# A recurrent block with routed experts on one core: the receptance product on VectorE in every step, row scatters in one run per step, expert slots starting two places earlier

## The reference

```python
xn = _layernorm(x, axis=-1)
s = _L0_attn_ref(xn, ...)            # recurrent block
g = _silu(_L0_ffn_ref(xn, ...))      # shared expert + one routed expert per token
x = x + s * g
...
# in _L0_attn_ref
k = einsum(xk, att_kw); v = einsum(xv, att_vw); sr = sigmoid(einsum(xr, att_rw))
rwkv = sr * _wkv(time_decay, time_first, k, v)     # the receptance product
x = x + einsum(rwkv, att_ow)
h = _ln(x, ln2_w, ln2_b)                            # second norm
kk = square(relu(einsum(xk, f_kw))); x = x + sigmoid(einsum(xr, f_rw)) * einsum(kk, f_vw)
# in _L0_ffn_ref: the shared swiglu of all tokens, and for each token
# the swiglu of the expert with the largest logit, on x * sigmoid(logit)
```

## Time and profile before

| | us |
|---|---|
| median of 3 runs | 498.06 |
| the profiled execution, its own time | 497.8 |
| its span, first to last instruction | 495.9 |
| TensorE (PE) busy | 444.2 |
| VectorE (DVE) busy | 406.5 |
| ScalarE (ACT) busy | 355.9 |
| GpSimd (POOL) busy | 282.2 |

### The profile page before, as it was taken

How to read it: one execution, slowest core, us unless ns; L and a number is a source line. 1 busy time by engine, 2 the same in 40 slices (tenths; PEclk the granted TensorE clock), 3 DMA queues, 4 the chain that set the end, 5 groups by cost and what they waited for, 6 DMA issues and landing times. The chain is left out here.

```text
span 495.9 us, 9005 instructions
## 1 busy us (share of the span) xinstructions
PE 444.2 (90%) x2663; PEld 332.7 (67%) x2663; DVE 406.5 (82%) x806; ACT 355.9 (72%) x716; POOL 282.2 (57%) x318
## 2 busy tenths in 40 slices
PE   1898998869989997799999999999999999988895
PEld 1667665547566663669686969687878787855562
DVE  4573969969799797979796979797988989789996
ACT  4868778564565657578787878787879697867891
POOL 7834685288787888427374655555555646470050
PEclk9999899898999999999999999999999999999999
DMA  8992000011511111225757565746573837209397
GB/s 255 273 275 51 2 0 1 5 45 57 190 35 48 46 33 51 55 81 151 212 156 214 172 208 171 232 138 206 147 237 108 226 101 224 79 19 291 106 123 217
DMA packets 66384, 64.97 MB, mean 131 GB/s; under 512 B 5952, under 2 KB 54465, under 8 KB 66256
## 3 DMA queue, kind: packets, MB, share of 16 engines
q1 hardware_dynamic: 58512, 53.52, 38.4%
q0 software_dynamic: 6960, 9.84, 7.3%
q10 hardware_dynamic: 864, 1.04, 0.7%
HBM read 46.86 MB, written 19.28 MB: 133 GB/s over the span
## 5 line engine op out<-in xcount | busy, mean ns | idle before, releaser
L1049 POOL DMA_INDIRECT routed_out<-xh,xs x71 | 93.1, 1312 | 45.2 <-ACT xh L809 30.5
L1041 POOL DMA_INDIRECT tokens_by_expert<-xn,pos x64 | 68.5, 1070 | 27.4 <-issue 27.4
L518 PEld LDWEIGHTS bank_ring<-xh,ew 128*128 128x128 f32 x568 | 70.2, 192 | 10.8 <-issue 9.7
L518 PE MATMUL bank_ring<-xh,ew 128*128 128x128 f32 x568 | 75.6, 276 | 1.0 <-ACT xh L809 0.5
L475 PE MATMUL bank_out<-fvw,kk 128*128 128x128 f32 x512 | 66.1, 277 | 0.0
L475 PEld LDWEIGHTS bank_out<-fvw,kk 128*128 128x128 f32 x512 | 62.0, 193 | 1.9 <-issue 1.9
L1318 DVE TENSOR_TENSOR kk<-rk 128x512 f32<-128x512 f32 x30 | 24.1, 804 | 40.9 <-ACT rk L767 40.7
L801 ACT ACTIVATE px<-bank_ring 128x256 f32<-128x256 f32 x71 | 27.1, 381 | 25.4 <-PE bank_ring L518 25.2
L532 PE MATMUL bank_ring<-ew,hx 128*128 128x128 f32 x284 | 43.5, 276 | 0.4 <-ACT xh L809 0.4
L532 PEld LDWEIGHTS bank_ring<-ew,hx 128*128 128x128 f32 x284 | 37.8, 193 | 0.6 <-ACT xh L809 0.6
L485 PEld LDWEIGHTS bank_ring<-sdn,hs 128*128 128x128 f32 x256 | 31.0, 192 | 10.3 <-issue 6.1
(11 more groups left out here) (198 smaller groups left out, 1096.8 us busy)
## 6 DMA issues: line engine op xcount, KB each, us to landing
ew<-ex_w SPq DMA_DIRECT2D x71, 384.0 KB
tokens_by_expert<-pad_row SPq DMA_DIRECT2D x1, 4686.0 KB, 21.1
xs<-tokens_by_expert SPq DMA_DIRECT2D x71, 66.0 KB, 3.0
xi<-x SPq DMA_DIRECT2D x12, 256.0 KB, 4.6
out<-xn SPq DMA_DIRECT2D x11, 256.0 KB, 4.0
ew<-routed_out SPq DMA_DIRECT2D x9, 256.0 KB, 4.4
out<-x SPq DMA_DIRECT2D x5, 256.0 KB
out<-xn POOLq DMA_DIRECT2D x5, 256.0 KB, 6.0
```

What stands on the lines that cost most here:

```text
L518: last = nc.tensor.matmul(part(GU[n % 2], q, P), part(w, q, P), xt[:, 0:P], start=True, stop=True)
L1041: nc.gpsimd.indirect_dma_start(xs_dram, bass.IndirectOffsetOnAxis(ap=POS[:, t:t + 1], axis=0), XN[:, t * XROW:(t + 1) * XROW], None).then_ ...
L1049: nc.gpsimd.indirect_dma_start(routed_dram, bass.IndirectOffsetOnAxis(ap=XS[(n - 2) % NXS][:, CH:CH + 1].bitcast(i32), axis=0), XH[n % NXH ...
```

## The change

Three edits. `make_rw` goes from GpSimd to VectorE in steps 1 to 14, between `running_max` and the second `ffn_square`. The scatters of a step become one run ahead of place 4: 10 in step 1 and 18 in each of the next three. Slots -2 and -1 move from place (5, 4) to (5, 2), and the others are spread from (5, 3) on instead of (5, 5): 77 places for 73 slots instead of 75.

```diff
     slots = [("E", n) for n in range(-2, XTILES + 2)]
-    steps[E_STEP][4] += slots[:2]
+    steps[E_STEP][2] += slots[:2]
     slots = slots[2:]
-    places = [(E_STEP, k) for k in range(5, 8)] + [(i, k) for i in range(E_STEP + 1, CHUNKS - 1) for k in range(8)]
+    places = [(E_STEP, k) for k in range(3, 8)] + [(i, k) for i in range(E_STEP + 1, CHUNKS - 1) for k in range(8)]
...
-            def make_rw(c):
-                pool.wait_ge(s_tn, c + 1)
-                pool.wait_ge(s_iq, c + 1)
-                if c > 0:
-                    pool.wait_ge(s_att, c)
-                nc.gpsimd.tensor_tensor(RW[:, :], NUM, LQ[:, :], ALU.mult).then_inc(s_rw, 1)
...
-                    scatter(9)
+                    scatter(10)
                 elif 0 < i <= E_STEP:
-                    scatter(12)
+                    scatter(18)
                 for k in range(4, 8):
                     fill(i, k)
-                if T:
-                    make_rw(i)
-                if 0 < i < E_STEP:
-                    scatter(5)
...
                 running_max(2)
+                make_rw(1)
                 ffn_square(0, 3)
...
                 if P1:
                     running_max(i + 1)
+                if T:
+                    make_rw(i)
                 if C:
                     ffn_square(i - 1, 3)
```

## The result

The kernel before took 497.47 us (495.76 to 499.38, 4 runs), the changed one 502.19 us (500.63 to 503.44, 4 runs). The ratio is 1.0094 [1.0053, 1.0136]. The forecast of 492.8 was wrong in its sign, and the time lies outside its range. The profiled execution of the changed kernel took 500.63 us (span 498.7), 2.8 more than the one of before.

What follows compares the result with a forecast made beforehand. TensorE, busy 90%, was to gain from its waits: a lead of 7.7 us by step 5, less 4.7 there, left 3.0; later slots 2.0, sum 5.0 of 497.8, forecast 492.8, range 490.0 to 497.5.

Steps and rivals of the forecast that it cites:

- Step 1, 3.5 and 0.4: End of step 1: product on VectorE removes TensorE's wait, gain 3.5 us; clock staying at 1.00 adds 0.4.
- Steps 2 and 3, 1.4 and nothing: Step 2: product falls into VectorE's idle time and the square's collision goes, gain 1.4 us; step 3 gives nothing.
- Step 4, 1.0 for z and 1.4 for the square: Step 4: TensorE's wait for z and some tenths behind it, 1.0 us; the square's collision with GpSimd's product, 1.4 us.
- the lead is not carried: Rival, chance 0.27: TensorE is full in steps 2 to 4, so only step 1's 3.5 is won; 495.3 us.
- GpSimd keeps pace, at most 1 to 2 us behind the statistics.: Steps sending rows: 18 scatters take about 24 us, x_sm and d 3 more, against steps of 25 to 27.8.
- the long runs of 12 keep 1.26: Argument against the rival that GpSimd falls behind: scatters in the kernel's long runs of 12 stay at 1.26 us.
- the lead of 7.7: Gain in us summed over steps 1 to 4, expected at transpose L400 of step 5, before step 5's give-back.
- The price: GpSimd's scatters: four products and gaps fewer, so the last scatter starts some 6 us earlier, near 191 instead of 197.52.
- the third rival: GpSimd falls behind, chance 0.06: scatters 0.2 us longer each, 3.8 slower, 501.6 us; decides from 0.13 more per scatter.
- The rule on the shared ports: VectorE and GpSimd lock shared ports: three products would each hold a scatter up to 0.69 us; forecast counted no cost.
- The slots, 4.7 in step 5: Step 5: slots moved earlier make TensorE stand; give-back 4.0 us plus a third of 2 us for half clock, 4.7.
- Later, two stretches with a slot fewer, 2.0: After step 5: two stretches between L429s lose a slot, 1.0 us each, gain 2.0, ends 0 and 2.9.

Runs made afterwards that it cites:

- d moved: Changed kernel with old slots, scatters 12, 17, 17, 18, and the time-mixing difference d of chunks 3 to 5 made by VectorE instead of GpSimd: 490.70 us, ratio 0.9872.
- the last two runs there: Chip S: product on VectorE, old slots, scatters 14, 17, 17, 16 (496.47 us); changed kernel with 14 then 17 scatters, step 10's empty place at 2 (498.43).
- the product alone: Kernel before with the product on VectorE, scatters in single runs of 14, 17, 17, 16, slots old: 515.10 us on chip P, 496.47 on chip S.

## Why the prediction was wrong

*Step 1, 3.5 and 0.4.* Right: 3.8 measured, no wait, no square of GpSimd's, clock 1.00.

*Steps 2 and 3, 1.4 and nothing.* Right in sum: 1.0 and 0.6. The products are hidden as said, and the squares are 0.69.

*Step 4, 1.0 for z and 1.4 for the square.* Right as a possibility: with GpSimd relieved (8 or 12 scatters a step, or d moved) steps 1 to 4 took 105.3 to 106.3 us, a lead of 6.7 to 7.8 where the forecast said 7.7. The rival "the lead is not carried", by which steps 2 to 4 would be full on TensorE, is thereby excluded.

*"GpSimd keeps pace, at most 1 to 2 us behind the statistics."* **This is the step that failed.** I counted 24 us for a run of 18, at 1.26 a scatter and with a slow first one, and 3 for x_sm and d, 27 in all; and compared them with steps of 25 to 27.8, where my own sum had just made steps 2 and 4 shorter, by 1.4 and 2.4. Measured, the three runs of 18 took 24.0, 26.0 and 23.4 us, and x_sm and d 4.5, 3.2 and 4.7: 28.6 a step on the mean. Nothing waits in between, so x_sm follows x_sm by 28.5, 29.2 and 28.1, 85.8 together, however fast the others are; steps 2 to 4 took 85.4. The rows of before had it. My argument that "the long runs of 12 keep 1.26" was a wrong reading: from start to start they have 1.38, 1.39 and 1.36 in steps 2 to 4. From the first scatter at 96.01 to the end of the last at 198.48 are 102.5 us, and 64 scatters with their gaps (85.8), three x_sm and d (10.9) and four products (5.8) fill them. GpSimd, 57% busy over the span, was full for those 102 us. Cutting 10, 18, 18, 18 out of 64 put the surplus into step 4; 14, 17, 17, 16 put it into step 2 (32.7); 12, 17, 17, 18 spread it, and 5.5 of the lead of 7.7 are there at step 5, with d moved 7.0.

*The price.* The last scatter started at 194.91, not at 191. I had the four products and their gaps at 6 us; they brought 4.6, since a gap of 0.30 takes the place of each. The first pass ended 0.7 earlier, and longer scatters (1.2) and longer x_sm and d (1.6) took 2.8 back. Step 4's stand of 3.14 and the half clock behind it took 6.2 (31.6 against 25.4), and of the lead of 7.7 at step 5 2.0 were left, 0.7 of them from the first pass. This is the mechanism of the third rival, to which I gave 0.06; it said it decides from 0.13 us more a scatter than 1.26. That is 1.39, which is what they took from start to start over the whole (1088 ns and the gap of 0.30), and in before 1.37. The condition of the rival was as good as met in the trace that I had. That its time of 501.6 comes out as well is luck: it counted 0.2 us more a scatter beside the product, and has nothing of the 2.9 us lost behind step 5.

*The rule on the shared ports.* I set it aside for two scatters of 0.95 and 0.96, and looked only at the new product. The traces bear the rule out, for all of VectorE's instructions with two SBUF inputs. All twenty traces together have 1280 scatters. Of the 554 that begin while VectorE is idle, or in one of its instructions that has a single input or an input in PSUM (a `bank`), none takes over 1.09 us. All 271 that take over 1.12 begin inside one with both inputs in SBUF (`den_num`, the scans of `bb_aa`, `xk`, `kk`, `rw`), and 249 of them are longer than 0.96 by what was left of it, less 0 to 0.25. Of the 299 that begin with 0.35 us or more of such an instruction left, only 53 are not longer, and those began within 0.05 us of its start. The Trainium skill, "SBUF — State Buffer", section "SBUF: two separate sides", has a lock between a VectorE operation with two SBUF inputs and a GpSimd one that reads SBUF; that these scatters are held by it agrees with the numbers above. The new product itself did little: one scatter in steps 2 to 4 begins inside it, that of step 3 at 155.88, 0.35 ahead of its end, and takes 1.18; the one at 129.96 in step 2 begins ahead of it and takes 0.96. But what scatters are held is 7.0 us over all 64 before and 8.2 after. An estimate from these rows: without what scatters and x_sm are held, 18 x 1.26 + 3.2 = 25.9 us a step would be GpSimd's work, less than the 26.8 and 27.0 of steps 2 and 3, and it would have kept pace. No run takes VectorE's instructions away, so this is read from rows and not tested. The reverse blocking, the square held up by GpSimd's product, was as read, and is gone.

*The slots, 4.7 in step 5.* Measured 3.9 against before; 4.1 on chip S, between the last two runs there; 5.7 on chip Q, between the changed kernel and before. Right in size, though for other reasons in part: TensorE had lost its lead by then and waited 1.41 for `xs`, not 4.

*Later, two stretches with a slot fewer, 2.0.* Wrong. Steps 6 to 14 took 228.0 on the mean of eight traces with the new slots (227.0 to 228.9) and 227.7 on ten with the old (226.7 to 229.6): nothing. In the changed kernel step 7 gained 2.1, step 12 0.2, and step 10 lost 3.2. The move of step 10's empty place stands in the text ahead of the prediction, and I gave it no price. With the slot back at place 1, two kernels took 225.6 and 226.1, 1.6 to 2.1 under that mean of 227.7, but only 1.1 under the product alone on the same chip: something of the 2.0 is there, its size is open, and the empty place 1 took it. How much that place costs varies: step 10 took 27.8 in three of the eight traces and 26.2 in the others.

*The account.* Forecast 492.8; 5.7 of the lead missing at the end of step 4, 0.8 less given back in step 5, 2.9 missing behind it: 500.6, where 500.63 was measured.

## What to carry to other kernels

An engine's share of the span hides the stretch in which it is full: for a queue that carries a fixed number of sends between two points, multiply its number by the mean of the group plus the gap (the distance of two neighbouring rows leaves out what other engines hold up), add all else on that engine in the stretch, and compare with the distance of the two points. If they are equal, that engine is the bound there, and work taken off it only helps as far as its runs are cut so that no other engine's input comes late. When an order is respread, every empty place moved has a price: ask which wait it uncovers.

## What the runs showed of the hardware

On three of the five chips of the experiments engines stood for 2 to 10 us with no releaser in the steps that send rows, in the kernel before too, and mostly at the same instructions: ScalarE's copy to xt in step 2 stood 5.1 to 6.6. In the two executions with 8 rows a step there were none in steps 2 to 4, beside the same loads of weights and at either place in the step; with 16 to 18 there were several in each profiled execution, and with the five loads moved away 3.8 to 5.3 were left at that copy. What makes the engines stand, whether instructions arrive late or something else, and why only there, stays open. It matters, since the same edit cost 0.9% where the first result was taken and 3.6% on chip Q.

A scatter takes 0.96 us, and 0.30 stand behind it; the longer ones, up to 2.11, are those that VectorE's instructions with both inputs in SBUF hold up (above). The first scatter behind GpSimd's d looks slow (1.87 in step 3 of the changed kernel) because VectorE is then often at `den_num`; in step 4, where VectorE stands idle, it takes 1.08 behind the same d. And TensorE's stands of 3.14 (step 4), 2.55 (step 10) and 4.47 (step 2 of the product alone) were each followed by some us at the 0.50 clock. The steps took 6.2, 2.7 and 5.8 us more than the same steps without the stand (25.4, 25.15 and 26.9): such a step lost between one and two times the length of its stand.
